# Patch filter and last spectral mixing of a four-layer spectral kernel: new division of work, new layout, three spectra buffers

## The reference, cut to what matters

```
x = x + L0(gn(x))   # spectral mixing on selected low frequencies
x = x + L1(gn(x))   # 8x8 patches: rfft2, times mask, times scaling, irfft2
x = x + L2(gn(x))   # 5x5 convolution with reflected border
x = x + L3(gn(x))   # rfft2 of x and of a 32x32x64x64 kernel, product summed over channels, irfft2
```

```
L1: mask     = radial gain curve on the 8x8 frequency grid
    edge     = sobel magnitude of the channel mean, averaged in every 8x8 patch, scaled to 0..1 per image
    scaling  = 1 + 0.5 * edge_norm * high_frequency_mask      # one number per image and patch
    out      = irfft2(rfft2(patch) * mask * scaling)
L3: x_f = rfft2(x); k_f = rfft2(weights)
    out_f = einsum('bchw,ochw->bohw', x_f, k_f); out = irfft2(out_f)
```

## Time and profile before

| what | value |
|---|---|
| median of 3 runs | 879.60 us (875.92 to 885.77) |
| the profiled execution | 882.25 us, span 880.4 us, mean granted clock 0.914 |
| busy: PE, DVE, ACT, POOL | 735.8, 576.8, 420.7, 120.0 us |
| patch filter, 331 to 408 us of the span | PE 60.4, DVE 61.7, ACT 41.4, POOL 40.5 us busy |
| mixing, 693.9 to 789 us of the span | PE 82.7, DVE 65.9, ACT 61.7 us busy |

### The profile page before, as it was taken

The page is one execution under the profiler, slowest core; times in us unless marked ns, Lnnn a source line. Parts: engine busy times, 40 slices in busy tenths (PEclk is TensorE's granted clock), DMA queues, the critical chain, the costliest instruction groups (busy, mean ns, idle before and its releaser), DMA issues. The chain is left out here.

```text
span 880.4 us, 27840 instructions
## 1 busy us (share of the span) xinstructions
PE 735.8 (84%) x11781; PEld 623.0 (71%) x11781; DVE 576.8 (66%) x1074; ACT 420.7 (48%) x727; POOL 120.0 (14%) x119
## 2 busy tenths in 40 slices
PE   7999997882588558785899999958999488879997
PEld 7999997882577337674444444428998488879997
DVE  3554452885849656887777777777775867746454
ACT  0132334782454006553699995004778267754200
POOL 0000001440000004552022313004320100000000
PEclk9999998996979668987999999987999699999995
DMA  8599987764020000000000000004000478830055
GB/s 312 197 369 322 338 247 223 165 139 113 6 55 3 1 1 2 0 0 0 2 1 2 1 1 1 1 1 96 2 2 8 90 158 177 175 64 1 2 193 194
DMA packets 48686, 80.70 MB, mean 92 GB/s; under 512 B 20162, under 2 KB 38472, under 8 KB 43736
## 3 DMA queue, kind: packets, MB, share of 16 engines
q1 hardware_dynamic: 31960, 62.65, 25.6%
q10 hardware_dynamic: 16640, 16.78, 5.6%
...
## 5 line engine op out<-in xcount | busy, mean ns | idle before, releaser
L1587 DVE SCALAR_TENSOR_TENSOR X<-bank,c_power,X 32x512 f32 x128 | 96.7, 755 | 36.5 <-PE bank L1537 32.9
L1738 PE MATMUL bank<-m_xp,m_kf 128*32 128x64 f32 x2048 | 82.8, 248 | 23.4 <-DVE m_xp L1673 11.1
L1738 PEld LDWEIGHTS bank<-m_xp,m_kf 128*32 128x32 f32 x2048 | 81.8, 171 | 24.5 <-issue 24.4
L421 DVE COPY ks_rows<-bank 128x512 f32<-128x512 f32 x64 | 41.2, 687 | 66.4 <-PE bank L351 66.4
L221 DVE BATCH_NORM_STATS2 bn<-X 128x6 f32 (+1 forms) x128 | 81.2, 682 | 2.9 <-POOL X L1327 1.6
L439 ACT COPY ks_spec<-bank 128x512 f32<-128x512 f32 x64 | 34.3, 589 | 93.8 <-PE bank L366 93.8
L1493 ACT ACTIVATE c_r<-X,c_nrm 32x1024 f32 (+1 forms) x56 | 75.0, 1340 | 2.4 <-DVE c_nrm L1561 1.1
L351 PE MATMUL bank<-ks_fw,ks_src 64*128 64x64 f32 x1024 | 68.7, 298 | 6.4 <-DMA ks_src<-in_L_conv_weights 6.4
L587 POOL TENSOR_SCALAR f_src<-X,rstd,shift 128x512 f32<-128x512 f32 x52 | 40.2, 776 | 238.2 <-POOLq L243 200.7
L351 PEld LDWEIGHTS bank<-ks_fw,ks_src 64*128 64x128 f32 x1024 | 68.1, 215 | 6.3 <-issue 6.3
L366 PE MATMUL bank<-ks_fh,ks_rows 64*128 64x128 f32 (+1 forms) x1152 | 71.2, 278 | 0.0
...
## 6 DMA issues: line engine op xcount, KB each, us to landing
...
```

Of the source, the lines that this page charges most:

```text
L421: dve.tensor_copy(rows[p][:, m, :, C // 2 * g + r:C // 2 * (g + 1):2], ps[2 * g + r][:].rearrange("p (c n) -> p n c", n=N)).then_inc(rows_ ...
L1587: dve.scalar_tensor_tensor(x, of.rearrange("p (y x) -> p y x", x=HN), filt.power[at, 2:3], x, ALU.mult, ALU.add).then_inc(added, 1)
L1738: last = pe.matmul(ps[4 * half + m // 8][at:at + C, m % 8 * N:(m % 8 + 1) * N], kf[p][:, j, :, H * half + m], xp[half][:, j, m].rearrange( ...
```

## The change

It has two parts, and they don't touch each other.

**Patch filter.** The stage is unrolled over 32 chunks; nothing stops between groups. A chunk is now 16 rows of 32 pixels (still 8 patches), and PE writes its products so that PSUM holds them in pixel order, in runs of 8 numbers. `edge` is widened to one number per pixel of a patch row, by two ACT and two DVE copies at the end of the edge stage. DVE makes two passes over each chunk: `p_tmp` = second product times edge, and X = X + first product, which now comes after POOL's add and also gives the sum of the chunk. bn_stats is gone; the sum of squares comes from one more pass, on DVE in chunks 1, 3 and 5 of each group (scalar_tensor_tensor) and on ACT in the other five (Square with a sum output). POOL normalises two chunks of eight, six chunks ahead, with ACT doing the others. There are three pairs of PSUM banks and three `p_tmp` instead of two. One reduction at the end gives all of `st`.

**Mixing.** `kf` is stored with real and imaginary parts apart, so that a block of spectra is filled by two DMAs of 1 MB, each to all 128 partitions. There are three blocks: two are loaded in the forward stage, the third as the mixing begins, the others when the unit pair three before is done. POOL clears both halves of `m_xp`, with a semaphore for each, and DVE clears nothing. The stage is unrolled. The scratch for dynamic DMAs is set to 2048.

```diff
-        self.kf = nc.dram_tensor("kf", (SLOT // 4, P, 2, C // IB, IB * N), F32, kind="Internal").ap()
+        self.kf = nc.dram_tensor("kf", (SLOT // 4, 2, P, C // IB, IB * N), F32, kind="Internal").ap()
...
-                            act.dma_start(pr.kf[:, :, part, n, :].rearrange("s p n -> p s n"),
+                            act.dma_start(pr.kf[:, part, :, n, :].rearrange("s p n -> p s n"),
...
+        def widen(copy, q):
+            of = ps[3 + 4 * (q // 2)][:, q * N:(q + 1) * N].rearrange("p (s c) -> p s c", c=PS)
+            return copy(edge[:, q].rearrange("p s (c x) -> p s c x", x=PS),
+                        of.unsqueeze(3).broadcast_to([P, PS, PS, PS]))
...
+                act.wait_ge(spread, 1)
+                for q in range(Q // 2):
+                    widen(act.copy, q)
...
-                    last = pe.matmul(ps[3][:, q * N:(q + 1) * N], spread_m[:, q * P:(q + 1) * P], eb[:],
+                    last = pe.matmul(ps[3 + 4 * (q // 2)][:, q * N:(q + 1) * N], spread_m[:, q * P:(q + 1) * P], eb[:],
...
-                dve.tensor_copy(edge[:].rearrange("p q n -> p (q n)"), ps[3][:, 0:Q * N])
+                for q in range(Q // 2, Q):
+                    widen(dve.tensor_copy, q)
...
+    UNITS, AHEAD, POOL_AHEAD, RING = NCH * Q, 3, 6, 3
...
+    def normal_by(n):
+        return {1: "dve", 2: "pool"}.get(n, "act") if n < POOL_AHEAD else "pool" if n % NCH in (2, 6) else "act"
+    def square_by(n):
+        return "dve" if n % NCH in (1, 3, 5) else "act"
...
+        src = pr.sb(ctx, "p1_src", [P, NCH, CH])
+        tmp = [pr.sb(ctx, f"p1_tmp{p}", [P, 2 * PS, HN]) for p in range(RING)]
+        waste = {e: pr.sb(ctx, f"p1_waste_{e}", [P, 2 * PS, HN]) for e in squared}
+        sums = pr.sb(ctx, "p1_sums", [P, Q, 2, NCH])
...
+        def block_of(n):
+            q, j = divmod(n, NCH)
+            rows, half = divmod(j, 2)
+            return pr.X[:, q, :].rearrange("p (s y x) -> p s y x", s=4, x=N)[:, rows, :, HN * half:HN * half + HN]
+        def result(n, t):
+            two = pr.banks[:, 2 + 2 * (n % RING):4 + 2 * (n % RING)]
+            return two.rearrange("p h (y t x) -> p t (h y) x", t=2, x=HN)[:, t]
+        def normalise(eng, e, n):
+            if n >= UNITS or normal_by(n) != e:
+                return
+            q, j = divmod(n, NCH)
+            if q:
+                eng.wait_ge(turned, n - NCH + 1)
+            to = src[:, j].rearrange("p (k y x) -> p k y x", k=4, x=PS)
+            of = block_of(n).rearrange("p y (k x) -> p k y x", x=PS)
+            scale, shift = pr.rstd[:, q:q + 1], pr.shift[:, q:q + 1]
+            if e == "act":
+                m = eng.activation(to, of, ACT.Identity, scale=scale, bias=shift)
+            else:
+                m = eng.tensor_scalar(to, of, scale, shift, ALU.mult, ALU.add)
+            m.then_inc(ready[e], 1)
             @block.tensor
             def _(pe):
-                pe.sem_inc(turned, START)
+                def turn(n):
+                    e = normal_by(n)
+                    pe.wait_ge(ready[e], count(normal_by, e, n + 1))
+                    if n >= 2:
+                        pe.wait_ge(turned_read, n - 1)
+                    for k in range(4):
+                        m = pe.transpose(ps[n % 2][:, k * P:(k + 1) * P], src[:, n % NCH, k * P:(k + 1) * P],
+                                         pr.ident[:])
+                    m.then_inc(turned, 1)
                 pr.keep_warm(pe, 6)
-                with pe.Fori(0, Q) as q:
-                    def turn(j):
-                        pe.wait_ge(ready, NCH * q + j + 1)
-                        if j >= 2:
-                            pe.wait_ge(turned_read, NCH * q + j - 1)
-                        for k in range(4):
-                            m = pe.transpose(ps[j % 2][:, k * P:(k + 1) * P],
-                                             src[:, (4 * j + k) * P:(4 * j + k + 1) * P], pr.ident[:])
-                        m.then_inc(turned, 1)
-                    turn(0)
-                    for j in range(NCH):
-                        if j + 1 < NCH:
-                            turn(j + 1)
-                        pe.wait_ge(turned_read, NCH * q + j + 1)
-                        if j == 0:
-                            pe.wait_ge(added, START + NCH * q)
-                        if j >= 2:
-                            pe.wait_ge(added, START + NCH * q + j - 1)
-                        for k in range(4):
-                            for h in range(2):
-                                at = slice(h * PS * PS, (h + 1) * PS * PS)
-                                m = pe.matmul(ps[2 + 2 * (j % 2) + h][:, k * P:(k + 1) * P],
-                                              tt[j % 2][at, k * P:(k + 1) * P], mm[at, :, at], start=True, stop=True)
-                        m.then_inc(filtered, 1)
+                turn(0)
+                for n in range(UNITS):
+                    if n + 1 < UNITS:
+                        turn(n + 1)
+                    pe.wait_ge(turned_read, n + 1)
+                    if n >= RING:
+                        pe.wait_ge(added, n - RING + 1)
+                    for k in range(4):
+                        for h in range(2):
+                            at = slice(h * PS * PS, (h + 1) * PS * PS)
+                            to = ps[2 + 2 * (n % RING) + h][:].rearrange("p (y t k x) -> p k t y x", t=2, k=4, x=PS)
+                            m = pe.matmul(to[:, k], tt[n % 2][at, k * P:(k + 1) * P], mm[at, :, at],
+                                          start=True, stop=True)
+                    m.then_inc(filtered, 1)
             @block.scalar
             def _(act):
+                def square(n):
+                    if square_by(n) == "act":
+                        q, j = divmod(n, NCH)
+                        act.wait_ge(added, n + 1)
+                        if count(square_by, "act", n):
+                            act.wait_ge(squared["act"], count(square_by, "act", n))
+                        act.activation(waste["act"][:], block_of(n), ACT.Square, scale=1.0 / N,
+                                       accum_out=sums[:, q, 1, j:j + 1]).then_inc(squared["act"], 1)
+                for n in range(AHEAD):
+                    normalise(act, "act", n)
+                for n in range(UNITS):
+                    act.wait_ge(turned, n + 1)
+                    if n >= 2:
+                        act.wait_ge(filtered, n - 1)
+                    act.copy(tt[n % 2][:], ps[n % 2][:]).then_inc(turned_read, 1)
+                    normalise(act, "act", n + AHEAD)
+                    if n >= AHEAD:
+                        square(n - AHEAD)
+                for n in range(UNITS - AHEAD, UNITS):
+                    square(n)
             @block.vector
             def _(dve):
+                def scale(n):
+                    q, j = divmod(n, NCH)
+                    dve.wait_ge(filtered, n + 1)
+                    if n >= RING:
+                        dve.wait_ge(finished, n - RING + 1)
+                    at = edge[:, q, :].rearrange("p (s h) x -> p s h x", h=2)[:, j // 2, :, HN * (j % 2):HN * (j % 2) + HN]
+                    dve.tensor_tensor(tmp[n % RING][:].rearrange("p (h y) x -> p h y x", h=2),
+                                      result(n, 1).rearrange("p (h y) x -> p h y x", h=2),
+                                      at.unsqueeze(2).broadcast_to([P, 2, PS, HN]), ALU.mult).then_inc(scaled, 1)
+                def add(n):
+                    q, j = divmod(n, NCH)
+                    dve.wait_ge(finished, n + 1)
+                    x = block_of(n)
+                    dve.scalar_tensor_tensor(x, result(n, 0), 1.0, x, ALU.mult, ALU.add,
+                                             accum_out=sums[:, q, 0, j:j + 1]).then_inc(added, 1)
+                def square(n):
+                    if square_by(n) == "dve":
+                        q, j = divmod(n, NCH)
+                        dve.wait_ge(added, n + 1)
+                        if count(square_by, "dve", n):
+                            dve.wait_ge(squared["dve"], count(square_by, "dve", n))
+                        dve.scalar_tensor_tensor(waste["dve"][:], block_of(n), 1.0 / PIX, block_of(n), ALU.mult, ALU.mult,
+                                                 accum_out=sums[:, q, 1, j:j + 1]).then_inc(squared["dve"], 1)
+                for n in range(AHEAD):
+                    normalise(dve, "dve", n)
+                for n in range(UNITS):
+                    scale(n)
+                    if n >= 2:
+                        square(n - 2)
+                    if n:
+                        add(n - 1)
+                add(UNITS - 1)
+                for n in (UNITS - 2, UNITS - 1):
+                    square(n)
+                dve.wait_ge(added, UNITS)
+                for e in squared:
+                    dve.wait_ge(squared[e], count(square_by, e, UNITS))
```

(71 more changed lines are left out.)

166 lines of the change are left out of this document (53 added, 113 removed).

## The result

The changed kernel takes **903.05 us** (median of 5, 898.63 to 917.24) against 879.6 for the kernel before (875.35 to 886.02, 5 runs beside it): ratio **1.026** [1.021, 1.032], slower, where 854 was predicted. The profiled execution took 916.77 us, 915.0 of them span. Some executions of each kernel get a lower granted clock near their end and take longer, this one too; ratios leave such executions out, and stages are compared up to 810 us of the span and not behind it. Four more runs of the changed kernel, on another chip, took 900.96 to 917.82 us where the kernel before took 879.55, and their profile has the same five waits for spectra, 43.7 us together instead of 44.0.

What follows compares the result with a forecast made beforehand. No single engine was taken to bound the whole; DVE bounded the inside of a filter group. From 882.25 us, 10.8 (filter) and 16.6 (mixing: 1.7 + 8.2 + 3.8 + 2.9) gave 854.9, or 852.2 from the median; forecast 854, range 844 to 866.

Steps and rivals of the forecast that it cites:

- Spectra: Mixing: loads to 128 partitions take 5 us a block instead of 10.5, so PE's 8.2 us of waits for spectra go.
- the old rate: Mixing: at some 200 GB/s, 10.5 us a block, five loads take 53 us against 58 us of matmuls, so are covered.
- the 8.2 us go: Mixing: PE's 8.2 us of waiting for spectra disappear, with or without the faster load rate.
- Spectra by 32 partitions: Mixing of the kernel before: four 32-partition DMAs run at some 200 GB/s with the DMA share at 0.98.
- The 3.8 issue pause is the loop's, and gone: Mixing: PE's 3.8 us "issue" pause, shortly before the loop turns back, was taken as the loop's and saved by unrolling.
- Rival 2: Unrolled mixing: PE runs out of instructions while spectra load; five loads cost 19 us, giving 874 us; chance 7%.
- The rule on taken branches: Mixing: a taken branch breaks sequential instruction prefetch and unrolled code avoids this, so the 3.8 us pause goes.
- Filter: Filter stage: 1.78 us a chunk, 10.8 us saved; bounds 1.68 us (13.9 saved) and 2.15 us (-0.7).
- the 1.76: Filter: POOL's chunk period if DVE's square and POOL's addition exclude each other: 1.47 + 3/8 x 0.60, plus 0.06 hand-over.
- Rival 1: Filter: DVE becomes the bound at 2.15 us a chunk, its gain is gone, giving 866 us; chance 12%.
- Rivals 3 and 4: Filter: PSUM runs of 8 slow the matmuls (886 us, 4%); Square needs another ACT table (899 us, 4%).
- Start of the mixing: Mixing: POOL's four memsets hold DVE's staging passes, PE starts at 692.2 instead of 693.9, saving 1.7 us; bounds 5.0 and 0.

Runs made afterwards that it cites:

- number 6: The changed kernel with `kf` laid out so a block of spectra is one DMA of 128 rows, stored by four DMAs a tile: 862.07 us, ratio 0.981.
- experiments 3 and 4: The changed kernel, same layout, each block by four loads of 32 partitions (878.39 us, ratio 0.992), or of 64 with slowest dimension 2 (1010.07 us).
- number 7: The kernel before with the changed filter and one-DMA loads of 128 rows, keeping its mixing loop and two buffers: 864.93 and 868.84 us, about 0.986.
- number 5: The changed kernel with four 32-partition loads a block, those issued during the mixing bringing 1/32 of their bytes: 852.67 us, ratio 0.971.

## Why the prediction was wrong

**Spectra: the step that failed.** It said that 128-partition transfers move 413 GB/s, as stage one's do, so 5 us a block, and that even at the old rate three buffers cover the loads. The row behind it was right, and number 6 does reach that rate. But I carried it over by the number of partitions alone and didn't look at the access pattern on the HBM side: the transfers of stage one read 128 equal rows, this one reads 4 by 32. It ran at 108 GB/s and 19.8 us a block; the floor I had set below ("the old rate", 10.5 us) was no floor. So "the 8.2 us go" became 44.0 us of waits. The Trainium skill, "DMA: Bandwidth & Descriptors", section "Why a DMA increments its semaphore by 16 and not by 1", says that the engine count is the largest number up to 16 that divides the slowest dimension of both patterns; the 2, 4 and 16 engines of experiments 3 and 4 agree. With the measured 19.8 us a block the five loads are 99 us against 58 of matmuls.

**Spectra by 32 partitions.** That four such loads run at some 200 GB/s was read rightly. The Trainium skill, "SBUF — State Buffer", section "Door 1: The DMA port swizzle (why `[64,N]` ≈ `[32,N]`)", gives a reason in partitions: 32 of them reach 8 of 16 ports and 16 reach 4, with limits of 218 and 109 GB/s. The 212 GB/s of 32 partitions agree with it; the 120 of 16 are 10% above its limit.

**"The 3.8 issue pause is the loop's, and gone".** Wrong in its reason, and right in the changed kernel by luck: its loads leave twelve engines free, and instructions come in time. The pause goes with the loads, in the loop as well (0.2 us in number 7), and returns fivefold in the unrolled list when loads hold all engines for 10 us. Rival 2 had the mechanism and the price (19 against 18.6). It got 7% because the other loads of the loop had cost no pause; but from 716 to 779 us the loop needed one packet of q8, where the unrolled list needs one for every unit, so those loads said nothing about it. The rule on taken branches that the prediction sets beside this rival didn't decide it: the unrolled list has the pauses.

**Filter: right, at its lower bound.** The period was 1.69 instead of 1.78, the lower bound 1.68, so the gain was 12.7 us instead of 10.8. PE's 1.68 was exact. The sum output costs DVE next to nothing: the pass with it starts at 343.98 and the next at 344.59, 0.61 apart, where up to 0.78 was allowed; its extra instruction of 0.08 us runs beside the next pass. The square on DVE and POOL's work do exclude each other, but at a price of 0.4 us in nine additions and 0.5 in three normalisations, where 0.60 was put down for each square. So POOL, busy 16.04 of 17.20 us, still fits and does not set the period, as the 1.76 had it. Rival 1 (DVE the bound) is out: DVE waits for PE.

**Rivals 3 and 4: out.** The filter's 16 matmuls take 1.16 us as before, though they write runs of 8 numbers; no table load stands in the stage.

**Start of the mixing: right.** Four memsets hold four DVE passes (2.30 to 2.02 us, then 0.41), and PE starts 11.6 us after the stage's start instead of 13.2: 1.6 saved, 1.7 predicted.

**The sum.** With the terms as measured where they work (12.8, and 17.4 in the mixing, by numbers 5 and 6) the kernel would be at 852, and number 5, whose loads cost next to nothing, is at 852.67. (The two numbers come from different chips, so how close they are is in part chance; its ratio of 0.971 gives 854.) So the two stages were costed rightly but for the loads: their rate, and what they do to PE's instructions. The range failed with it: its lower case allowed 9 us of gain in the mixing, and no case had loads slower than before, though the pattern of the loads was itself part of the change.

The best that compute the reference whole are number 6 (0.981) and the filter alone (0.985), the latter with no change of layout. Both beat either kernel, by 1 to 2% where the kernel before is concerned. The rest, some 10 us, would need loads of 128 rows without the long issues of the stores; whether there is a layout of `ks_spec` on the chip that gives both wasn't tried.
